# Experts' lists: the places of the eight largest are found after the search, in the waits of the merge

## The reference, cut to what matters

```python
n_tokens, n_experts = 2048, 16
capacity = 128                                  # tokens that each expert takes
xn = xf / rms * norm_weight
logits = xn @ router_weight.T + router_bias     # 2048 x 16
probs = softmax(logits)
_, idx = top_k(logits.T, capacity)              # per expert: the 128 tokens with the largest logits
xe = xn[idx]                                    # gathered, then fc1, gelu, fc2
gates = take_along_axis(probs.T, idx, axis=1)
output = zeros(2048, 256).at[idx.reshape(-1)].add(y * gates)   # divided by the sum of gates
```

## Time and profile before

| what | value |
|---|---|
| runs | 888.73, 891.49, 894.78 us; median 891.49 |
| span of the profiled execution | 891.9 us |
| the lists' block, first instruction to `idx` | 179.9 to 235.8 us |
| of this the search, first MAX8 to the issue of the lists' DMA | 183.77 to 205.82 us |
| wait for the lists | 2.58 us |
| merge | 208.38 to 219.2 us |
| counting and slots | 219.2 to 235.3 us |

### The profile page before, as it was taken

The page is one execution under the profiler, slowest core; times in us unless marked ns, Lnnn a source line. Parts: engine busy times, 40 slices in busy tenths (PEclk is TensorE's granted clock), DMA queues, the critical chain, the costliest instruction groups (busy, mean ns, idle before and its releaser), DMA issues. The chain is left out here.

```text
span 891.9 us, 14491 instructions
## 1 busy us (share of the span) xinstructions
PE 690.8 (77%) x4387; PEld 629.7 (71%) x4388; DVE 473.4 (53%) x1100; ACT 289.2 (32%) x642; POOL 351.7 (39%) x467
## 2 busy tenths in 40 slices
PE   1777777500699999379999999945489889999992
PEld 1677667400698889338788888724489889999991
DVE  3343455387211111167877777758267558666661
ACT  1243444100033333143333333233245425443430
POOL 2221302000144545403343344224375566766854
PEclk9757585655699999779999999976699999999996
DMA  8770670030079995359210000020343351222322
GB/s 258 115 178 10 155 274 0 8 113 3 13 217 313 306 320 144 73 170 369 69 37 18 18 18 0 24 71 0 121 126 93 73 138 27 39 45 43 43 36 35
DMA packets 78034, 91.77 MB, mean 103 GB/s; under 512 B 9248, under 2 KB 69024, under 8 KB 77856
## 3 DMA queue, kind: packets, MB, share of 16 engines
q1 hardware_dynamic: 63808, 74.40, 27.8%
q0 software_dynamic: 11536, 14.13, 9.3%
q10 hardware_dynamic: 2640, 2.62, 0.9%
HBM read 75.58 MB, written 16.17 MB: 103 GB/s over the span
## 5 line engine op out<-in xcount | busy, mean ns | idle before, releaser
L1350 PE MATMUL f_pt<-xparts,cparts 128*128 128x512 f32 x480 | 119.2, 398 | 0.0
L1887 ACT ACTIVATE nh<-npH,c_sb 128x288 f32<-128x288 f32 x128 | 64.1, 501 | 120.0 <-PE npH L1859 119.7
L1350 PEld LDWEIGHTS f_pt<-xparts,cparts 128*128 128x128 f32 x480 | 88.7, 191 | 18.4
L1801 POOL DMA_INDIRECT out<-nyg,si x51 | 86.7, 1700 | 19.2 <-issue 18.6
L108 POOL TENSOR_TENSOR held<-ones 128x1 f32<-128x1 f32 x136 | 47.7, 351 | 113.1 <-DVE nyg L1906 52.2
L1338 POOL TENSOR_TENSOR hidl<-sums,hidh 128x512 fp32r<-128x512 f32 x40 | 52.1, 1303 | 93.3 <-ACT hidh L1392 93.3
L1857 PE MATMUL npH<-nxh,w1l 128*128 128x288 f32 x256 | 78.1, 305 | 1.6 <-DVE nxl L1899 1.6
L1868 PE MATMUL npY<-nhh,w2l 128*128 128x288 f32 x256 | 77.8, 304 | 0.0
L1870 PE MATMUL npY<-nhh,w2h 128*128 128x288 f32 x256 | 76.5, 299 | 0.0
L1859 PE MATMUL npH<-nxh,w1h 128*128 128x288 f32 x256 | 76.4, 299 | 0.0
L1869 PE MATMUL npY<-nhl,w2h 128*128 128x288 f32 x256 | 76.2, 298 | 0.0
(11 more groups left out here) (344 smaller groups left out, 1501.9 us busy)
## 6 DMA issues: line engine op xcount, KB each, us to landing
w_sb<-in_w SPq DMA_DIRECT2D x32, 1024.0 KB, 8.3
w_sb<-in_v SPq DMA_DIRECT2D x16, 1024.0 KB, 9.8
bias_sb<-in_bias SPq DMA_DIRECT2D x4, 1024.0 KB, 14.0
acc<-zrow SPq DMA_DIRECT2D x1, 2056.0 KB, 23.7
sums<-acc SPq DMA_DIRECT2D x4, 514.0 KB, 5.4
x_sb<-in_x SPq DMA_DIRECT2D x1, 2048.0 KB, 10.0
table<-row ACTq DMA_DIRECT2D x1, 2048.0 KB, 18.9
b_sb<-in_b SPq DMA_DIRECT2D x1, 2048.0 KB, 8.7
```

What stands on the lines that cost most here:

```text
L1350: ins = pe.matmul(pp[:, c % 2], cparts[:, u, wn, at], xparts[:, xn, k, chunk], start=(k == 0 and (wn, xn) == (0, 1)), stop=(k == KD - 1 an ...
L1801: pool.indirect_dma_start(result, bass.IndirectOffsetOnAxis(ap=si3[:, s:s + 1], axis=0), yg[:, s], None, bounds_check=B * N - 1, oob_is_er ...
```

## The change

`chunk` gets 16 buffers, one for each round, so that the values a round looked at are kept. A round is then `max` and `match_replace` alone, and the last has no `match_replace`; `SORTED` becomes 31. The function `places_of(rounds)` issues the `max_index` of the rounds named, each counted on `step` and none waited for. It is called six times: for five rounds behind the search, one behind `least`, two behind the counts, two behind the shares that partitions give, and six behind `place`. The CAST to `pickf` and the addition move behind the last of these. On TensorE the transposition of `pickf` moves behind the 16 products that fill `pr`, with a step of its own; VectorE copies `pickT` and `mineT` after the second of four `hot` instructions, and TensorE waits for that copy (`turned_at`) before the products with `hot`.

```diff
-                chunk = sb("chunk", [P, 2, CW], into=ph)
+                chunk = sb("chunk", [P, CAP // 8, CW], into=ph)
...
-                SORTED = 3 * CAP // 8
+                SORTED = 2 * (CAP // 8) - 1
...
                         for r in range(CAP // 8):
                             now = slice(8 * r, 8 * r + 8)
-                            at, other = chunk[:, r % 2], chunk[:, 1 - r % 2]
-                            link(dve.max(best[:, now], at))
-                            put(dve.max_index(pick[:, now], best[:, now], at))
-                            link(dve.match_replace(other, best[:, now], at, -3e38))
-
+                            link(dve.max(best[:, now], chunk[:, r]))
+                            if r + 1 < CAP // 8:
+                                link(dve.match_replace(chunk[:, r + 1], best[:, now], chunk[:, r], -3e38))
+
+                        def places_of(rounds):
+                            for r in rounds:
+                                now = slice(8 * r, 8 * r + 8)
+                                put(dve.max_index(pick[:, now], best[:, now], chunk[:, r]))
+
+                        places_of(range(0, 5))
 
                         dve.wait_ge(lists_in, 16)
...
-                        put(dve.tensor_copy(pickf[:], pick[:]))
+                        places_of(range(5, 6))
                         dve.wait_ge(pe_step, 1)
...
-                        link(dve.tensor_scalar(pickf[:], pickf[:], num[:, BASE:BASE + 1], None, ALU.add))
-                        table_steps.append(steps[0])
+                        places_of(range(6, 8))
 
                         dve.wait_ge(pe_step, 2)
...
+                        places_of(range(8, 10))
                         dve.wait_ge(c_step, 7)
                         dve.wait_ge(pe_step, 3)
...
-                        dve.wait_ge(pe_step, 4)
-                        put(dve.tensor_copy(pickT[:], pv[:, P:2 * P]))
-                        link(dve.tensor_copy(mineT[:], pv[:, 2 * P:3 * P]))
+                        places_of(range(10, 16))
+                        dve.wait_ge(step, steps[0])
+                        link(dve.tensor_copy(pickf[:], pick[:]))
+                        link(dve.tensor_scalar(pickf[:], pickf[:], num[:, BASE:BASE + 1], None, ALU.add))
+                        table_steps.append(steps[0])
                         for q in range(4):
...
-                        table_steps.append(steps[0])
+                            table_steps.append(steps[0])
+                            if q == 1:
+                                dve.wait_ge(pe_step, 9)
+                                put(dve.tensor_copy(pickT[:], pv[:, P:2 * P]))
+                                link(dve.tensor_copy(mineT[:], pv[:, 2 * P:3 * P]))
+                                table_steps.append(steps[0])
                         put(dve.memset(idx[:], 0))
 
-                        dve.wait_ge(pe_step, 9)
+                        dve.wait_ge(pe_step, 10)
...
-                        least_set, counted_at, pickf_set, taken_at, placed, hot_set = table_steps
+                        least_set, counted_at, taken_at, placed, pickf_set, *hot_at = table_steps
+                        turned_at = hot_at.pop(2)
...
-                        pe.transpose(pv[:, P:2 * P], pickf[:], ident[:])
                         pe.wait_ge(step, placed)
                         pe.transpose(pv[:, 2 * P:3 * P], place[:, 1], ident[:]).then_inc(pe_step, 1)
...
+                        pe.wait_ge(step, pickf_set)
+                        pe.transpose(pv[:, P:2 * P], pickf[:], ident[:]).then_inc(pe_step, 1)
+                        pe.wait_ge(step, turned_at)
                         for e in range(E0):
                             if e % 4 == 0:
-                                pe.wait_ge(step, hot_set - 3 + e // 4)
+                                pe.wait_ge(step, hot_at[e // 4])
```

## The result

The changed kernel takes 885.64 us (median of 20 runs, 879.97 to 893.06), the kernel before 891.52 us (20 runs, 885.77 to 897.66). The ratio is 0.9939, its 95% interval 0.9919 to 0.9959: 5.4 us less, between 3.7 and 7.2 us. The forecast was 885.5 us in a range of 881.5 to 889.8.

The account below looks back on a forecast made before the run. The prediction took VectorE's search, heading the chain through the experts' lists stage, to bound the kernel. Its terms, -7.16 + 0.15 + 1.05 = -5.96 us, took 891.49 to 885.5 us, range 881.5 to 889.8.

Parts of the forecast that it names:

- What bounds the kernel: Experts' lists stage: one chain, VectorE's until 219.2 us, then TensorE's; a microsecond out of the search moves everything behind it.
- The search gets shorter: First MAX8 to the lists' DMA: rounds without places fall from 1.38 to 0.96 us, the search from 22.05 to 14.89.
- The low end (6.71): Search gain if the replacement's pair needs 0.08 us spacing instead of 0.05, making a round 0.99 us.
- Pieces 2, 3 and 4: One place behind `least` and two behind the counts, free; two before the wait for line 947, costing 0.15 us.
- Piece 5: Six places behind `place`: with CAST and addition 3.19 us until `pickf` is ready and `hot` starts, covered by line 952.
- Piece 1: Five places behind the search: 2.19 us (high 2.55) inside the 2.56 us wait for the lists, free.
- signs of being wrong: Round above 1.0 us, merge over 2.6 us behind the issue, late `hot`, or clock of 0.50 on line 974.
- What the end of the chain pays: Moved transposition and copies before the products with `hot`: line 959 starts 1.05 us later (0.8 to 1.4).
- The clock did not fall in the gap: Rival: TensorE's idle 0.6 us between lines 952 and 959 drops its clock, losing 4.0 us, 889.5 us; chance 0.06.
- the slower case: Rival: lines 952 and 959 never get the full clock, losing 6.6 us, 892.1 us; chance 0.04.
- The whole pair: Rival: 0.51 us leaves each search round, making it 0.87 us, search gain 8.51 us, time 884.3 us; chance 0.08.
- the gain was not hidden elsewhere: Rival: something else sets the start of the expert blocks, so the time stays at 891.5 us; chance 0.03.

Follow-up runs that it names:

- its repetition: The changed kernel once more, without an edit: 883.82 us against 891.62, ratio 0.9936 (0.9899 to 0.9973).
- early_turn: Against the changed kernel, the transposition of `pickf` stands behind twelve of the sixteen products that fill `pr`, not all: 884.05 us, ratio 0.9909.
- wide_gap: Against the changed kernel, `pickT` and `mineT` are copied four times instead of once, widening TensorE's gap to 2.22 us: stage 49.14 us.

## Why the prediction was right, point by point

**What bounds the kernel.** That a microsecond out of the search is a microsecond of the kernel held: 5.39 and 5.76 us less in the stage in two profiles, 5.4 and 5.7 us by the two ratios (0.0061 of 891.52 and 0.0064 of 891.62). The ratios' intervals are wide, 3.7 to 7.2 us for the first, so the times agree with this but could not show it to less than a microsecond. That the median lies 0.1 us from the forecast is luck: the terms below miss by 0.2 to 0.6 us each, in both directions.

**The search gets shorter.** Forecast 7.16 us, measured 22.05 - 15.21 = 6.84. The low end (6.71) had the right reason: the replacement's pair takes the wider spacing once it follows MAX8 itself, 0.08 us, and the round is 0.984 us.

**The places come back.** Pieces 2, 3 and 4 held, the fourth at less than the 0.15 us taken: from `least` to `place` nothing is lost (6.31 us against 6.33). Piece 5 held: 3.08 us to the first `hot` instead of 3.19, and covered. Piece 1 was called free at both ends, and that failed. The five places do fit into the wait, but with them the wait is longer, by 0.58 us in the profile after and 0.28 in its repetition (1.06 and 0.76 us of idle time were left of it instead of about 0.4), and a merge later than 2.6 us behind the issue was among the prediction's own signs of being wrong. I had asked only whether the work is over before the DMA lands, not what else moves on the DMA engines by then: a packet of program code goes ahead of one engine's share of the lists.

**What the end of the chain pays.** Forecast 1.05 us; the slots took 0.89 and 0.83 us longer than before. The clock rose earlier in both profiles, so that the row of line 964 took 5.01 and 4.95 us instead of 5.14; without that it is 1.02 us in both, so the term held. early_turn shows it for itself: 0.64 to 0.70 us go away when the turn is hidden, about 0.9 at the same clock.

**The sum.** -6.84 + 0.58 - 0.02 + 0.89 = -5.39 us in the profile after, -6.84 + 0.28 - 0.03 + 0.83 = -5.76 in its repetition, -5.96 forecast. The two misses, 0.3 us in the search and 0.3 to 0.6 in the wait, were partly made up by piece 4, which cost nothing, and by the end, where the earlier clock was chance.

**The rivals.** The clock did not fall in the gap of 0.65 us. The prediction read from the fall 1.1 us behind the last product that a short idle time can be enough; the rows do not show that, since the fall came 6.8 us behind the rise with a gap or without one. wide_gap shows what a long gap costs: the second row then ends after the fall. The stretch got its full clock (1.00 from 221.0), so the slower case did not come. The whole pair did not leave the round: it lost 0.395 us, even less than the 0.42 forecast. The Trainium skill's plain rule in "VectorE: DVE Perf Modes", section on the DRAIN, that the next operation waits for an empty pipe, holds here only with the exception that the same section names: a MATCH_VALUE_LOAD starts at 198.13, before FIND_INDEX8 (197.80 + 0.42 = 198.22) has ended, and a place in a row costs 0.394 us where its own rows sum to 0.49. And the gain was not hidden elsewhere.

## What to carry to other kernels

A result that only later steps need does not belong in a chain where each step waits for the one before; keep its inputs (here sixteen small buffers) and find it where the engine idles anyway. Work is free in a wait only if what is waited for does not come later, so look at the wait's length after the change, and at what else the DMA queues carry in it, and not only at whether the work fits: here three places were free and five were not, by where a fetch of program code fell. When a transposition or copy is moved behind a row of products, put it inside the row, with enough products behind it to cover the copies.

## What the runs showed of the hardware that I had not expected

- A DMA of 64 KB from one SBUF tile to another landed 0.3 to 0.8 us later in the eight profiles in which a packet of 8 KB of program code started 1.33 to 1.43 us behind its issue: that packet held one of the 16 DMA engines for 0.47 to 0.73 us, and nine packets of the lists waited for it. A packet of that queue started whenever VectorE had begun 653 to 657 of its instructions, and it depends on the work in the wait whether this happens before the lists land.
- The stretch in which TensorE was granted its full clock began 2.5 to 3.7 us behind the start of the same row of products and lasted 6.8 us in all fourteen profiles, with 0 to 2.22 us of idle time in it. With 2.22 us it ended in the midst of the second row, while TensorE was busy.
- In code that is the same, from `idx` to the end, single executions differ by up to 13.5 us (649.5 to 663.0), more than twice what this change gains: the stage's own stretch in the trace shows a change of 0.6 us that 10 runs of the whole don't.
